# Eleven late stages in one pipeline, and half of a spectrum product on GpSimd

## The chip, the core and the metric

The kernel runs on one core of a Trainium2 chip. The metric is the device time of one execution in microseconds; three runs of the kernel before gave 946.32, 946.88 and 947.59, so the median is 946.88. The core has a matrix engine (TensorE, PE), VectorE (DVE), ScalarE (ACT), GpSimd (POOL) and a queue for transfers (SyncE, SP). Each engine runs its own list of instructions strictly in the order in which it is written. Semaphores carry the dependencies: an instruction that waits holds up everything behind it on its engine.

## The reference

The input is x, 8 samples of 512 positions by 128 channels, float32. Four blocks follow each other, each of the form x = x + layernorm(block(layernorm(x))):

```
# 1: six layers, per layer:
q, k, v = heads(ln(x) @ wq), heads(ln(x) @ wk), heads(ln(x) @ wv)
x = (softmax(q) @ (softmax(k, over positions).T @ v)) @ wo + bo + x
x = leaky_relu(ln(x) @ w1) @ w2 + x
# 2: spiking feed-forward
y = relu(x @ W_fc.T) ** 2 @ W_proj.T
out = (how often a leaky accumulator of y fires in 5 steps) / 5
# 3: a state space convolution
u = (x @ Win.T + bin).T
k = einsum(C * B * dt, exp(-exp(-A_log) * dt * t))     # a kernel of 512 taps per channel
y = irfft(rfft(u, 1024) * rfft(k, 1024))[:512] + u * Dp
out = y.T @ Wout.T + bout
# 4: a gate over a time shift
xr, xk = mu_r * x + (1 - mu_r) * x_prev, mu_k * x + (1 - mu_k) * x_prev
out = sigmoid(xr @ W_r.T) * (relu(xk @ W_k.T) ** 2 @ W_v.T)
```

## The kernel before

A sample is a tile of 128 partitions by 512 (four blocks of 128). Three loops follow each other.

`layers` runs 51 steps. Step n begins item n (48 items: 6 layers by 8 samples), and at the same time carries items n-1, n-2 and n-3 through their later parts, so that the two matrix products with w1 (`h`) and w2 (`y`) of one item lie beside the attention of another.

`pipeline(6, spiking)` runs 14 steps. It holds block 2, and the start of block 3 (u and its eight bands, `butterfly`) for one sample per step. The convolution's own kernel is made here and in the layers: exponents on VectorE (L1144) and ScalarE (L883) in the layers' steps 8 to 24, 64 small products on TensorE (`kernel_slices`) in this loop's first two steps, and its spectrum (`spectrum`) in steps 3 to 10.

`slots` runs 17 steps with up to eight stages in each. It holds the rest of block 3 (`forward`, `inverse`, `out_proj`) and block 4. The transform `forward` takes four samples at a time, so that its products are 512 wide; its four multiplications, its subtraction and its addition per quarter (L1343 to L1349) are all on VectorE.

A normalisation runs over three engines: statistics on VectorE (`stats`), four or two tiny operations on GpSimd with a power among them (`rstd`, L680 to L683, and `mean_rstd`, L688 to L691), and the scaling on ScalarE (`normalise` L856, `scaled` L898). GpSimd adds the result to x (`add_to_x`, L775). Matrix products stand in line 358 and transposes in line 368 of the profile, whatever calls them.

## Time and profile before

| | |
|---|---|
| median of 3 runs | 946.88 us |
| profiled execution: its time, its span | 947.66 us, 945.9 us |
| TensorE busy | 816.8 us (86%) |
| VectorE busy | 703.6 us (74%) |
| ScalarE busy | 598.7 us (63%) |
| GpSimd busy | 424.9 us (45%) |
| granted TensorE clock, mean | 0.927 |

The span is what the trace covers; the time of the execution is 1.8 us more. The page gives busy time per engine for the whole span, and the kernel has parts with different limits, so the windows below part it: layers in their steady state, and all that lies behind them. A row of a timeline gives the start, the time from the first start to the last end of what it merges, and in brackets how long the engine had been idle and what ended that.

### The profile page before, as it was taken

The page shows a single profiled execution, that of the slowest core. Times are in us where ns is not written, and L with a number is a line of the kernel's source. Part 1 is how long each engine was busy: PE and PEld are TensorE (multiplying, and loading weights), DVE is VectorE, ACT ScalarE, POOL GpSimd, SP SyncE. Part 2 cuts the span into 40 slices and gives each one's busy share as a digit, 9 for nine tenths or more (in the row PEclk, how much of TensorE's full clock was granted, in tenths as well). Part 3 has the DMA queues.
Part 4 walks back from the last instruction along what each step waited for, and adds up shares of the span by engine and source line. Part 5 has one row for each costly group of instructions (what it writes and reads, how often), then busy time and mean ns, then how long its engine had stood idle before and what let it go on. Part 6 is the DMA issues. An engine that isn't in the chain of part 4 may idle for free.

```text
span 945.9 us, 15397 instructions
## 1 busy us (share of the span) xinstructions
PE 816.8 (86%) x5085; PEld 689.2 (73%) x5092; DVE 703.6 (74%) x2019; ACT 598.7 (63%) x1275; POOL 424.9 (45%) x706
## 2 busy tenths in 40 slices
PE   2688999999999999999999999989878766888543
PEld 2577878888888888888888888889657643646432
DVE  5788888888888888888888887620456789689843
ACT  3366767777777777777777677531778751236554
...
DMA packets 19726, 13.65 MB, mean 14 GB/s; under 512 B 2488, under 2 KB 18495, under 8 KB 19647
## 3 DMA queue, kind: packets, MB, share of 16 engines
...
## 4 chain that ended last, share of the span: by engine, by line
PE 65%; DVE 13%; ACT 9%; POOL 6%; issue 5%; DMA 0%; POOLq 0%; DVEq 0%; ACTq 0%
PE PS L358 58%; PE PS L368 7%; ACT XR L898 2%; POOL R L683 1%; ACT HL L982 1%; ACT XR L856 1%; ACT EK L856 1%; DVE ST L1098 1%; POOL RSTD L741 1%; DVE STATS L1191 1%; ACT HL L986 1%; DVE XI L1184 1%; POOL QB L757 1%; POOL RSTD L735 1%; POOL X L775 1%
## 5 line engine op out<-in xcount | busy, mean ns | idle before, releaser
L358 PE MATMUL PS<-W,HL 128*128 128x128 f32 x1536 | 201.7, 275 | 0.0
L358 PEld LDWEIGHTS PS<-W,HL 128*128 128x128 f32 x1536 | 193.4, 191 | 8.2
L919 ACT ACTIVATE HL<-PS 128x512 f32<-128x512 f32 x192 | 109.4, 594 | 22.7 <-PE PS L358 18.2
L724 POOL TENSOR_TENSOR JOIN<-STATS 128x8 f32<-128x8 f32 (+1 forms) x50 | 12.9, 257 | 220.5 <-DVE STATS L1191 220.5
L368 PE MATMUL PS<-ID,XR 128*128 128x128 f32 x448 | 73.2, 288 | 33.2 <-ACT XR L856 17.1
L358 PE MATMUL PS<-X2H,W1L 128*128 128x512 f32 x192 | 88.6, 461 | 5.9 <-issue 4.4
L368 PEld LDWEIGHTS PS<-ID,XR 128*128 128x128 f32 x448 | 53.0, 146 | 53.7 <-ACT XR L898 20.1
L939 ACT ACTIVATE EK<-PS,NKM 128x512 f32<-128x512 f32 x48 | 33.1, 689 | 88.1 <-DVE NKM L1261 88.1
L1191 DVE BATCH_NORM_STATS2 STATS<-XI 128x6 f32<-128x128 f32 x384 | 82.5, 278 | 0.3
L763 POOL TENSOR_TENSOR QB<-QB,QRC 128x512 f32<-128x512 f32 x48 | 51.0, 1062 | 69.6 <-DVE QRC L1295 69.6
L898 ACT ACTIVATE XR<-XI,RSTD 128x128 f32<-128x128 f32 x192 | 61.5, 393 | 29.9 <-POOL RSTD L741 29.6
L358 PE MATMUL PS<-X2H,W1H 128*128 128x512 f32 x192 | 75.8, 395 | 0.0
L358 PE MATMUL PS<-X2L,W1H 128*128 128x512 f32 x192 | 75.7, 394 | 0.0
L680 POOL TENSOR_SCALAR VE<-MV 128x4 f32<-128x4 f32 x56 | 13.5, 241 | 124.7 <-DVE MV L1102 68.5
L741 POOL TENSOR_TENSOR RSTD<-JOIN,MHALF 128x4 f32<-128x4 f32 x48 | 64.8, 1349 | 0.1
L358 PE MATMUL PS<-MM,QS 128*128 128x128 f32 x384 | 56.0, 290 | 9.1 <-DVE MM L1242 5.9
L683 POOL TENSOR_TENSOR R<-VE,MHALF 128x4 f32<-128x4 f32 x56 | 58.9, 1053 | 4.7
L358 PEld LDWEIGHTS PS<-MM,QS 128*128 128x128 f32 x384 | 48.1, 197 | 16.8 <-issue 8.5
L1271 DVE STREAM_TRANSPOSE QB<-QF 128x512 f32<-128x512 f32 x48 | 34.1, 711 | 32.9 <-ACT QF L851 32.9
L757 POOL TENSOR_TENSOR QB<-QB,QMX 128x512 f32<-128x512 f32 x48 | 51.1, 1064 | 5.1 <-DVE QMX L1273 5.1
L358 PE MATMUL PS<-EKT,XR 128*128 128x128 f32 x384 | 51.9, 279 | 1.6 <-ACT EKT L851 1.6
L1236 DVE TENSOR_TENSOR XR<-XI,RSTD 128x512 f32<-128x512 f32 x48 | 51.2, 1067 | 0.1
...
## 6 DMA issues: line engine op xcount, KB each, us to landing
...
QKV<-in_qkv SPq DMA_DIRECT2D x6, 192.0 KB, 2.9
...
```

The lines of the kernel that those rows point to most:

```text
L358: return nc.tensor.matmul(o, l, r, start=start, stop=stop, skip_group_check=True)
L368: last = nc.tensor.transpose(o[:, j * P:(j + 1) * P], i[:, j * P:(j + 1) * P], ID[:, :])
L683: return pool.tensor_tensor(r[:, :], ve[:, :], MHALF[:, 0:TILES], ALU.pow)
L741: pool.tensor_tensor(RSTD[:, 0:TILES], JOIN[:, 4, 0:TILES], MHALF[:, 0:TILES], ALU.pow).then_inc(s["ln1_rstd"], 1)
L757: pool.tensor_tensor(heads(QB[:, :]), heads(QB[:, :]), QMX[:, :].unsqueeze(2).broadcast_to([P, 32, DH]), ALU.subtract).then_inc(s["q_sub"], 1)
L763: pool.tensor_tensor(heads(QB[:, :]), heads(QB[:, :]), QRC[:, :].unsqueeze(2).broadcast_to([P, 32, DH]), ALU.mult).then_inc(s["q_nrm"], 1)
L898: last = nc.scalar.activation(o[:, j * P:(j + 1) * P], tile(src, b, j), ACT.Copy, scale=r[:, first + j:first + j + 1])
L919: nc.scalar.activation(HL[f][:, :], pH[f % 2][:, :], ACT.Prelu, alpha=LEAK).then_inc(s["hl"], 1)
L939: nc.scalar.activation(EK[:, :], pK[:, :], ACT.Exp, bias=NKM[:, 0:1], accum_out=KSM[:, 0:1]).then_inc(s["ek"], 1)
L1191: last = nc.vector.bn_stats(STATS[:, first + j, :], tile(XI, b, j))
L1236: tt(tiles(XR2[:, :]), tiles(seq(XI, before(b, 2))), per_tile(RSTD[:, TILES:2 * TILES]), ALU.mult).then_inc(s["xr2"], 1)
L1271: nc.vector.transpose(QB[:, :], QF[:, :]).then_inc(s["q_blk"], 1)
```

## The change

The two loops behind the layers are replaced by one. It has eleven stages, and sample v is in stage k at step 48 + v + k; the first three stages lie in the layers' last three steps, and `late` runs steps 51 to 65. This text calls a step of it t, with t = n - 48, from 0 to 17. The feed-forward of block 2 uses the layers' own `h` and `y` and their normalisation (stages 0 to 3); SPIKE is stage 4, STATE (normalise and transpose for block 3) 5, CONV (u, bands, transform, products) 6, BACK (inverse transform, projection, normalise) 7, SHIFT (normalise and transpose for block 4) 8, GATE 9 and FINISH 10. The constants:

```diff
-CHUNKS = {TABLES + 1 + i: i for i in range(PAIRS // 4)}
-
-SLICES = {0: range(0, 36), 1: range(36, PAIRS)}
-SPECTRUM = {3: (0, 1), 4: (2, 3), 6: (4,), 7: (5,), 8: (6,), 9: (7,), 10: (8,)}
-
-FIRST_SPECTRA = {BATCH + 3: (0, 1), BATCH + 4: (2,), BATCH + 5: (3,)}
-INVERSE, PROJECT, NORM, LN, TURN, MIX, GATE, FINISH = range(8)
-
-STARTS = [0, 1, 2, 3, None, None, 4, 5, 6, 7]
+ADD, PART, TURN, FFN, SPIKE, STATE, CONV, BACK, SHIFT, GATE, FINISH = range(11)
+def sample(n, stage):
+
+    v = n - ITEMS - stage
+    return v if 0 <= v < BATCH else None
+def late(step):
+    for n in range(ITEMS + 3, ITEMS + BATCH + FINISH):
+        step(n)
+CHUNKS = {0: (range(0, 3), range(3, 7)), 1: (range(7, 12), range(12, 16))}
+SLICES = {1: ((0, 8), (8, 14), (14, 20)), 2: ((20, 28), (28, 36), (36, 44)), 3: ((44, 51), (51, 58), (58, 64))}
+CENTRE, CENTRE_IN = ITEMS - 6, ITEMS - 5
+SPECTRUM = {ITEMS - 4: (0, 1, 2, 3), ITEMS - 3: (4, 5, 6, 7), ITEMS - 2: (8,)}
...
```

On TensorE the transform takes one sample, the time shift moves behind the matrices (W times a mix of x and x_prev becomes two products with prepared matrices), and one step is written as follows:

```diff
+def transform(v, n):
+    pe.wait_ge(s["bands"], v + 1)
+    pe.wait_ge(s["kf"], 3)
...
+    for half, bank in enumerate((pK, pW)):
+        for k in range(TILES):
+            for j in range(2):
+                last = mm(bank[:, k * P:(k + 1) * P], FWD[:, j * BINS * P + half * SEQ + k * P:][:, 0:P],
+                          V[:, (2 * k + j) * P:(2 * k + j + 1) * P], j == 0, j == 1)
+        last.then_inc(s["f_ps"], 1)
...
+def key_and_gate(v, n):
...
+    mm(pXT[:, :], WK1[:, :], SH[:, 1:1 + SEQ], True, False)
+    mm(pXT[:, :], WK2[:, :], SH[:, 0:SEQ], False, True).then_inc(s["k2_ps"], 1)
...
+    for j in range(TILES):
+        mm(pQ[:, j * P:(j + 1) * P], SH[:, 1 + j * P:1 + (j + 1) * P], WR1[:, :], True, False)
+        last = mm(pQ[:, j * P:(j + 1) * P], SH[:, j * P:(j + 1) * P], WR2[:, :], False, True)
+    last.then_inc(s["r_ps"], 1)
...
+def late_step(n):
...
+    if conv is not None:
+        project_in(conv, n)
+    if has_m:
+        h(m, 2)
+        y(m, 0)
+    if back is not None:
+        inverse(back)
+    if has_m:
+        y(m, 1)
+        h(m, 3)
+    if gate is not None:
+        key_and_gate(gate, n)
+    if has_m:
+        y(m, 2)
+    if has_x:
+        second_turn(n)
+    if has_m:
+        y(m, 3)
+    if spike is not None:
+        count(spike, n)
+    if conv is not None:
+        transform(conv, n)
+    if gate is not None:
+        value(gate)
+    if back is not None:
+        project_out(back, n)
+    if state is not None:
+        state_turn(state, n)
+    if has_x:
+        h(m + 1, 0)
+    if shift is not None:
+        shift_turn(shift, n)
+    if has_x:
+        h(m + 1, 1)
+late(late_step)
...
```

On GpSimd the convolution kernel's exponents move into the first two steps of the layers, and two of four multiplications of the spectrum come from VectorE, after a copy by ScalarE (`IMAG`):

```diff
+decay()
+exponents(0)
+input_rstd(0)
+exponents(1)
+exponents(2)
+join(0, TILES, 0)
+ln1_power(0)
+input_rstd(1)
+input_rstd(2)
+for p4 in range(3, 7):
+    exponents(p4)
...
+    if n == 0:
+        for p4 in range(7, 9):
+            exponents(p4)
+    if has_n:
+        pool.wait_ge(s["q_rec"], n + 1)
+        pool.tensor_tensor(heads(QB[:, :]), heads(QB[:, :]), QRC[:, :].unsqueeze(2).broadcast_to([P, 32, DH]),
+                           ALU.mult).then_inc(s["q_nrm"], 1)
+    if n == 0:
+        for p4 in range(9, PAIRS // 4):
+            exponents(p4)
+    if n + 3 < BATCH:
+        input_rstd(n + 3)
...
+def late_step(n):
...
+    if shift is not None:
+        pool.wait_ge(s["o_z"], shift + 1)
+        add_to_x(shift, ZOUT[:, :]).then_inc(s["o_x"], 1)
+    if state is not None:
+        pool.wait_ge(s["cnt_z"], state + 1)
+        add_to_x(state, ZCNT[:, :]).then_inc(s["cnt_x"], 1)
+    if shift is not None:
+        pool.wait_ge(s["sh_var"], shift + 1)
...
+        rstd_mean(3, EPS).then_inc(s["sh_nm"], 1)
+    if state is not None:
+        pool.wait_ge(s["st_var"], state + 1)
...
+        rstd(1, EPS).then_inc(s["st_rstd"], 1)
+    join_next(n)
+    if n + 1 < ALL:
+        ln1_power(n + 1)
+    if finish is not None:
+        pool.wait_ge(s["rv_z"], finish + 1)
+        add_to_x(finish, MEM[:, :]).then_inc(s["done"], 1)
+    if spike is not None:
+        pool.wait_ge(s["cnt_var"], spike + 1)
...
+        rstd_mean(0, EPS * STEPS * STEPS).then_inc(s["cnt_nm"], 1)
+    if conv is not None:
+        pool.wait_ge(s["imag"], conv + 1)
...
+        pool.tensor_tensor(PI[:, :], IMAG[:, :], KIM[:, :], ALU.mult).then_inc(s["turned"], 1)
+        pool.tensor_tensor(PR[:, :], IMAG[:, :], KRB[:, :], ALU.mult).then_inc(s["turned"], 1)
+    if gate is not None:
+        pool.wait_ge(s["rv_var"], gate + 1)
...
+        rstd_mean(4, EPS).then_inc(s["rv_nm"], 1)
+    if back is not None:
+        pool.wait_ge(s["o_var"], back + 1)
...
+        rstd_mean(2, EPS).then_inc(s["o_nm"], 1)
+late(late_step)
...
```

On ScalarE the six loads for the convolution kernel are issued first, before any other work, and a late step is written as follows:

```diff
+for t, d in ((ALOG, alog), (DTR, dtr), (IOTA, iota), (BMAT, bmat), (CMAT, cmat), (DP, dp)):
+    act.dma_start(t[:, :], d).then_inc(s["ssm_in"], 16)
+act.wait_ge(s["ssm_in"], SSM_LOADS)
+nc.scalar.activation(LA[:, :], ALOG[:, :], ACT.Exp, scale=-1.0).then_inc(s["la_exp"], 1)
+keys_high(0)
...
+def late_step(n):
...
+    if has_m:
+        hl(m, 0)
+        hl(m, 1)
+        hl(m, 2)
+    if finish is not None:
+        act.wait_ge(s["rv_nm"], finish + 1)
...
+        normalise(MEM[:, :], ACC[:, :], RS[4], NMS[4]).then_inc(s["rv_z"], 1)
+    if back is not None:
+        act.wait_ge(s["inv_ps"], back + 1)
...
+        copy(YR[:, :], pW[:, 2 * P:4 * P])
+        copy(YS[:, :], pK[:, 2 * P:4 * P]).then_inc(s["second"], 1)
+    if has_m:
+        hl(m, 3)
+    if state is not None:
+        act.wait_ge(s["st_rstd"], state + 1)
...
+        scaled(XS, state, 0, X, RS[1]).then_inc(s["st_x"], 1)
+    if gate is not None:
+        act.wait_ge(s["k2_ps"], gate + 1)
+        nc.scalar.activation(RK[:, :], pXT[:, :], ACT.Relu).then_inc(s["r_relu"], 1)
+        act.wait_ge(s["r_relu"], gate + 1)
...
+        nc.scalar.activation(SQ[:, :], RK[:, :], ACT.Square).then_inc(s["r_sq"], 1)
+        act.wait_ge(s["r_ps"], gate + 1)
...
+        nc.scalar.activation(SIG[:, :], pQ[:, :], ACT.Sigmoid).then_inc(s["r_sig"], 1)
+    if has_x:
+        second_copy(n)
+    if shift is not None:
+        act.wait_ge(s["sh_nm"], shift + 1)
...
+        normalise(ZN[:, :], lambda j: tile(X, shift, j), RS[3], NMS[3]).then_inc(s["sh_z"], 1)
+    if has_m:
+        act.wait_ge(s["y_ps"], (m + 1) * FB)
...
+        copy(YM[:, :], pY[:, :]).then_inc(s["ym"], 1)
+    if spike is not None:
+        act.wait_ge(s["cnt_nm"], spike + 1)
...
+        normalise(ZCNT[:, :], pQ[:, :], RS[0], NMS[0]).then_inc(s["cnt_z"], 1)
+    if state is not None:
+        act.wait_ge(s["st_T_ps"], state + 1)
...
+        copy(XTS[:, :], pX2[:, :]).then_inc(s["st_T"], 1)
+    if shift is not None:
+        act.wait_ge(s["sh_T_ps"], shift + 1)
+        act.wait_ge(s["sh0"], 1)
...
+        copy(SH[:, 1:1 + SEQ], pX2[:, :]).then_inc(s["sh_T"], 1)
+    if conv is not None:
+        act.wait_ge(s["f_ps"], 2 * conv + 2)
...
+        copy(IMAG[:, :], pW[:, :]).then_inc(s["imag"], 1)
+    if back is not None:
+        act.wait_ge(s["o_nm"], back + 1)
...
+        normalise(ZOUT[:, :], YO[:, :], RS[2], NMS[2]).then_inc(s["o_z"], 1)
+    if n + 1 < ALL:
+        next_input(n)
+late(late_step)
...
```

On VectorE:

```diff
+def products(v):
+    yr, yi = YF[:, 0:SEQ], YF[:, SEQ:2 * SEQ]
+    dve.wait_ge(s["f_ps"], 2 * v + 1)
...
+    tt(yr, pK[:, :], KRE[:, :], ALU.mult).then_inc(s["f_part"], 1)
+    tt(yi, pK[:, :], KIM[:, :], ALU.mult).then_inc(s["f_part"], 1)
+    dve.wait_ge(s["f_part"], 2 * v + 2)
+    dve.wait_ge(s["turned"], 2 * v + 2)
+    tt(yr, yr, PI[:, :], ALU.subtract)
+    tt(yi, yi, PR[:, :], ALU.add).then_inc(s["spectra"], 1)
...
+def late_step(n):
...
+    if has_x:
+        second_scale(n)
+    if n < ALL:
+        add_norm(n)
+    if shift is not None:
...
+        stats(lambda j: tile(X, shift, j), 3).then_inc(s["sh_var"], 1)
+    if state is not None:
...
+        stats(lambda j: tile(X, state, j), 1).then_inc(s["st_var"], 1)
+    if n <= ALL:
+        part_stats(n)
+    if conv is not None:
+        bands(conv)
+    if spike is not None:
+        spikes(spike)
+    if back is not None:
+        back_bands(back)
+    if has_x:
+        second_low(n)
+    if spike is not None:
...
+        stats(lambda j: pQ[:, j * P:(j + 1) * P], 0).then_inc(s["cnt_var"], 1)
+    if n + 2 < ALL:
+        first_stats(n)
+    if gate is not None:
...
+        tt(ACC[:, :], pXT[:, :], SIG[:, :], ALU.mult).then_inc(s["rv"], 1)
...
+        stats(lambda j: ACC[:, j * P:(j + 1) * P], 4).then_inc(s["rv_var"], 1)
+    if back is not None:
...
+        tt(tiles(YO[:, :]), tiles(pXT[:, :]), BOUT[:, :].unsqueeze(1).broadcast_to([P, TILES, P]),
+           ALU.add).then_inc(s["o_sum"], 1)
...
+        stats(lambda j: YO[:, j * P:(j + 1) * P], 2).then_inc(s["o_var"], 1)
+    if conv is not None:
+        products(conv)
+late(late_step)
```

`hl` of a late item is now a Relu and a Square. `next_input` scales XR for the coming step. The 64 small products of the convolution kernel lie in the layers' steps 1 to 3, its spectrum in steps 44 to 46, the centring of two matrices in 42 and 43. The names of the order below: BIG holds V, YF, ZCNT, ZOUT, ZN, XS, XTS, YT, YO, RK, SQ, SIG, PI and PR in the kernel after, QF holds YM, QS holds IMAG and EK holds MEM.

ScalarE, the end of a spiking step before (it ends with the normalisation of the spike count, EK):

```order
L898 ACTIVATE QS<-X,R 128x128 x4
L982 ACTIVATE HL<-PS 128x512
L986 ACTIVATE HL<-HL 128x512
L898 ACTIVATE XR<-X,R 128x128 x4
L982 ACTIVATE HL<-PS 128x512
L986 ACTIVATE HL<-HL 128x512
L851 ACTIVATE X2H<-PS 128x512
L851 ACTIVATE XTF<-PS 128x512
L856 ACTIVATE XR<-XI,NM,R 128x128 x4
L851 ACTIVATE YM<-PS 128x512
L856 ACTIVATE EK<-PS,NM,R 128x128 x4
```

ScalarE, the end of step t = 9 after: the spike count's normalisation, the transposed state (BIG<-PS), SH, IMAG (QS<-PS), the normalisation of block 3's output (BIG<-BIG), and then the next step's first Relu and Square:

```order
L828 ACTIVATE BIG<-PS,NM,R 128x128 x4
L823 ACTIVATE BIG<-PS 128x512
L823 ACTIVATE SH<-PS 128x512
L823 ACTIVATE QS<-PS 128x512
L828 ACTIVATE BIG<-BIG,NM,R 128x128 x4
L883 ACTIVATE HA<-PS 128x512
L886 ACTIVATE HL<-HA 128x512
L883 ACTIVATE HA<-PS 128x512
L886 ACTIVATE HL<-HA 128x512
```

What moved: between two feed-forward pairs now stand the end of five samples' stages, and the last of them waits for GpSimd.

GpSimd, the layers' step 0 into step 1, before (QB is the softmax of q, JOIN the statistics of the next step):

```order
L763 TENSOR_TENSOR QB<-QB,QRC 128x512
L711 TENSOR_SCALAR VEX<-MVX 128x4
L714 TENSOR_TENSOR RX<-VEX,MHALF 128x4
L705 TENSOR_TENSOR W1L<-W,W1H 128x512
L724 TENSOR_TENSOR JOIN<-STATS 128x8
L725 TENSOR_TENSOR JOIN<-STATS 128x8
L727 TENSOR_TENSOR JOIN<-JOIN 128x8
L728 TENSOR_SCALAR JOIN<-JOIN 128x8
```

GpSimd, the same place after:

```order
L754 TENSOR_TENSOR QB<-QB,QRC 128x512
L664 TENSOR_TENSOR BIG<-LA,IOTA 128x512 x7
L685 TENSOR_SCALAR VEX<-MVX 128x4
L688 TENSOR_TENSOR RX<-VEX,MHALF 128x4
L679 TENSOR_TENSOR W1L<-W,W1H 128x512
L698 TENSOR_TENSOR JOIN<-STATS 128x8
```

What moved: seven exponents, each 128 by 512 (BIG<-LA,IOTA), stand between the end of step 0 and the statistics of step 1.

## Rows read from the trace of the kernel before

**Rows 1.** Windows: stretch, its us, busy us (x instructions) of each engine, clock, DMA share, GB/s.
```profile
19.85:62.90 43.05, 30.19 (x139) 23.88 (x138) 34.36 (x104) 20.17 (x44) 20.71 (x33) 0.72 0.19 61
...
112.00:590.00 478.00, 472.21 (x3269) 414.24 (x3268) 396.66 (x949) 360.31 (x747) 233.19 (x374) 1.00 0.03 8
...
627.00:946.00 319.00, 229.79 (x1116) 176.77 (x1121) 202.20 (x774) 158.67 (x368) 131.31 (x224) 0.82 0.03 7
```

**Rows 2.** Waits of 673 to 946 us: waiter, released by: us in all, times, longest.
```profile
PE PS L358 <- ACT EK L856: 18.5, 7, 4.4
```

**Rows 3.** Timeline, ScalarE, 715 to 738 us: start, us, instruction, idle before.
```profile
720.84 1.50 ACT L856 ACTIVATE EK<-PS,NM,R 128x128 f32<-128x128 f32 x4
...
725.30 0.60 ACT L982 ACTIVATE HL<-PS 128x512 f32<-128x512 f32 x1 [2.96 <-PE PS L358]
...
725.93 0.63 ACT L986 ACTIVATE HL<-HL 128x512 f32<-128x512 f32 x1
...
735.34 1.50 ACT L856 ACTIVATE EK<-PS,NM,R 128x128 f32<-128x128 f32 x4
```

**Rows 4.** Timeline, TensorE, 728 to 731 us.
```profile
728.30 1.05 PE L358 MATMUL PS<-PROJ,HL 128*128 128x128 f32 x8
...
729.11 0.48 PE L358 MATMUL PS<-X2H,FCL 128*128 128x512 f32 x1
...
729.89 0.60 PE L368 MATMUL PS<-ID,QS 128*128 128x128 f32 x4
...
730.32 0.94 PE L358 MATMUL PS<-PROJ,HL 128*128 128x128 f32 x7
```

**Rows 5.** Timeline, GpSimd and VectorE, 720 to 724 us.
```profile
720.54 1.27 POOL L775 TENSOR_TENSOR X<-X,XR 128x512 f32<-128x512 f32 x1 [3.51 <-ACT XR L856]
...
720.91 1.18 DVE L1209 TENSOR_TENSOR FLY<-U 128x256 f32<-128x256 f32 x1
...
722.01 0.41 DVE L1210 TENSOR_TENSOR FLY<-U 128x256 f32<-128x256 f32 x1
```

**Rows 6.** Timeline, GpSimd, the first 36 us.
```profile
5.18 0.19 POOL L711 TENSOR_SCALAR VEX<-MVX 128x4 f32<-128x4 f32 x1 [3.90 <-DVE MVX L1178]
...
28.86 1.06 POOL L763 TENSOR_TENSOR QB<-QB,QRC 128x512 f32<-128x512 f32 x1 [5.38 <-DVE QRC L1295]
...
35.62 0.21 POOL L724 TENSOR_TENSOR JOIN<-STATS 128x8 f32<-128x8 f32 x1 [2.71 <-DVE STATS L1191]
```

**Rows 7.** The page, part 6: one DMA issue, KB, us to landing.
```profile
QKV<-in_qkv SPq DMA_DIRECT2D x6, 192.0 KB, 2.9
```

**Rows 8.** Groups of instructions: line, form, count, busy us, mean ns, idle before.
```profile
L358 PE MATMUL PS<-CE,BIG 128*128 128x8 f32 x128 | 27.0, 357 | 0.4 <-ACT WINC L851 0.4
```

**Rows 9.** Timeline, VectorE line 1299 (second residual), single instructions.
```profile
119.33 0.63 DVE L1299 TENSOR_TENSOR XI<-PS,XI 128x512 f32<-128x512 f32 x1
...
170.69 0.63 DVE L1299 TENSOR_TENSOR XI<-PS,XI 128x512 f32<-128x512 f32 x1
...
218.16 0.63 DVE L1299 TENSOR_TENSOR XI<-PS,XI 128x512 f32<-128x512 f32 x1
...
267.19 0.63 DVE L1299 TENSOR_TENSOR XI<-PS,XI 128x512 f32<-128x512 f32 x1
...
627.26 0.69 DVE L1299 TENSOR_TENSOR XI<-PS,XI 128x512 f32<-128x512 f32 x1 [6.46 <-PE PS L358]
```

**Rows 10.** Timeline, TensorE, VectorE and GpSimd, 924 to 940 us.
```profile
924.47 1.92 PE L358 MATMUL PS<-QS,WKT 128*128 128x512 f32 x2
...
936.16 0.69 DVE L1481 TENSOR_TENSOR ACC<-PS,QB 128x512 f32<-128x512 f32 x1 [3.75 <-ACT MEM L856]
...
936.88 0.87 DVE L1098 BATCH_NORM_STATS2 ST<-ACC 128x6 f32<-128x128 f32 x4
...
938.25 0.19 POOL L680 TENSOR_SCALAR VE<-MV 128x4 f32<-128x4 f32 x1 [0.88 <-DVE MV L1102]
...
939.92 0.19 POOL L691 TENSOR_SCALAR NM<-NM 128x4 f32<-128x4 f32 x1
```

More of the change, by code:

```diff
@@ L1 @@
+import itertools
 import numpy as np
@@ L29 @@
 ITEMS = LAYERS * BATCH
+ALL = ITEMS + BATCH
 def spike_levels():
@@ new lines, in second_turn, with kernel_slices @@
+            def second_turn(n):
+                pe.wait_ge(s["xr2"], n - 1)
+                if passed(n - 1, SHIFT):
+                    pe.wait_ge(s["sh_T"], passed(n - 1, SHIFT))
+                transposes(pX2, XR2).then_inc(s["x2T_ps"], 1)
+            def kernel_slices(first, end):
+                pe.wait_ge(s["bm_out"], 1)
+                pe.wait_ge(s["ce1"], 1)
+                pe.wait_ge(s["e2"], -(-end // 4))
+                for i in range(first, end):
+                    last = mm(pW[:, i * 8:i * 8 + 8], E2[:, i * P:(i + 1) * P], CE1[:, i * 8:i * 8 + 8])
+                if end == PAIRS:
+                    last.then_inc(s["k_ps"], 1)
```

1142 lines of the change are left out of this document (441 added, 701 removed).

## The prediction

> **What bounds the kernel now.** I read windows first, then waits, then timelines. The layers' steady state is bound by TensorE: in 112 to 590 us it is busy 472 of 478 us at full clock [rows 1]. So there work taken from VectorE or ScalarE gives nothing, and work added to TensorE costs its full length. The last residual of the layers is added at 627.3 us [rows 9], which leaves 318.6 us of the span of 945.9. There no engine is full: TensorE 230 of 319 us at a clock of 0.82, VectorE 202, ScalarE 159, GpSimd 131 [rows 1]. That part is bound by chains through four engines in fixed order. The plainest one: in the spiking steps TensorE waits 18.5 us in seven steps for ScalarE's normalisation of the count [rows 2]; one such normalisation starts at 720.84 and the next at 735.34, so a step is 14.5 us, although no engine has 14.5 us of work in it [rows 3]. By hand that chain is: normalisation 1.5, two products with FCH until the first Relu can start 0.8, four pairs of Relu and Square at 1.26, two scalings of about 1.3, two copies and YM at 0.6, a normalisation of 1.6: 13.3 us. The trace has 14.5, 9% more, from hand-overs and from TensorE at its lower level of 1.2 GHz after an idle stretch (ScalarE waits 2.96 us for the first h there). I keep this 9% as the surcharge on every chain below.
>
> **What the change does, by part.** I split it into the front (to the last residual) and the late part.
>
> Front, first normalisation. GpSimd starts it at 5.18 us [rows 6]. Now `decay` and one exponent come first. They wait for six loads from ScalarE's queue; a load lands some 2.9 us after its issue [rows 7], and with six issues in a row that is an estimated 6.2 us. Then an Exp, seven small GpSimd operations (0.2 to 0.3 each, 1.9) and an exponent of 1.06, the time of a 128x512 operation with a broadcast operand on GpSimd (QB in [rows 6]): 9.5 us. Nothing covers it, since everything waits for the first sample: +4.3.
>
> Front, step 1. The softmax product ends at 29.9 and the statistics are joined at 35.6 [rows 6]. Seven exponents (7.4) then stand in between, with the input's power (1.2) and W1L (1.6): 29.9 + 10.2 = 40.1 against 35.6, less what small slack VectorE has (0.5): +4.0. Behind this GpSimd work wait q_sub, the power for XR, and through them TensorE's next transposes.
>
> Front, the 64 small products. They take 27.0 us at the low clock (0.42 each) [rows 8], and about half of that at the high one. They move into steps 1 to 3, where TensorE is busy 30.2 of 43.1 us [rows 1]: 13 idle us, but in short waits on the path. Bounds: 0 if all fits, 14 if none. I take +5, and nothing back for a warmer clock. In step 6 the butterfly of the taps comes onto a VectorE that has little slack there: +1.5.
>
> Front, steps 42 to 46. 18 products of 128x128 for the spectrum (0.20 each, from four in 0.81 [rows 4]), one 512 wide (0.85) and one small, on a full TensorE: 4.7, and 0.6 for three copies ahead of GT on ScalarE: +5.3.
>
> Front, what goes. The steps that held the decay took 51.4 us for four steps (119.33 to 170.69), the same four of the next layer 49.0 [rows 9]: -2.3. The other exponents lay in steps bound by TensorE: 0. Sum of the front: 4.3 + 4.0 + 5 + 1.5 + 5.3 - 2.3 = +17.8; bounds +8 and +27.
>
> Late part. It replaces 31 steps by 18, of which 3 lie beside the layers' end. Loads of the fullest step, t = 9: VectorE about 22 us, TensorE about 22, ScalarE 19, GpSimd 19. But the order closes one cycle through all of it. From the end of a first Square (H): h and y 1.6; `inverse`, eight products of twice the width, 3.2; y, h 1.6; `key_and_gate` 2 x 0.85 + 8 x 0.20 = 3.3; y, transposes, y 2.05; count 1.2; `transform` 16 x 0.20 = 3.2; `value` 0.8; ACC on VectorE 0.7 (`project_out` writes the bank that ACC reads); `project_out` 0.8; state transposes, h, shift transposes 0.43 + 0.78 + 0.43 (TensorE in [rows 4], ACC in [rows 10]). That is 20.1. Then ScalarE: SH 0.6 and IMAG 0.6, for IMAG stands behind SH and so behind the shift transposes, though `transform` ended 5 us earlier. GpSimd: two products of 1.27 [rows 5], then, in its order, the gate's `rstd_mean` and the output's, 1.85 each (938.25 to 940.1) [rows 10]. ScalarE: ZOUT 1.6, and only then the next step's Relu and Square 1.26 [rows 3], for which TensorE's h waits. Sum 31.5 with hand-overs of 1 us: 9 us over the load of any engine.
>
> The other steps by the same walk: t = 3 only h, y and X2: 8.7. t = 4, 5, 6: the count's statistics (1.25), `rstd_mean`, ZCNT and XR stand between y and the next Relu: 14, 14.5, 15. t = 7 and 8: `back_bands` (four of 0.41, six of half that: 2.8) stands on VectorE behind `bands` (3.2 by the same rows, [rows 5]) and the five thresholds (1.8), and `transform` waits for it: 26, 25.5. t = 9: 31.5. t = 10: 29. From t = 11 there is no feed-forward, and the cycle goes on from ZOUT through `add_to_x` and the statistics to `bands`: 27, 25.5, 23.5. t = 14: 12.5. Tail of the last sample: add and statistics 2.5, `rstd_mean` 1.85, normalise, transpose, SH 2.7, `key_and_gate` at 1.2 GHz (WKT once takes 1.7 there [rows 10], so 3.4 + 3.4), `value` 1.1, and ACC to the end of the span 945.9 - 936.16 = 9.7 [rows 10]: 25. Head, from 627.3 to the first Square: 2. Sum 280; with 9%: 305 in place of 318.6, a gain of 13.5. Bounds: 280 with no surcharge; 330 with 18%, if TensorE falls to 1.2 GHz in each long gap of t = 4 to 6 and 11 to 13.
>
> The two spectrum products on GpSimd. VectorE's product takes 0.7 and its multiplications at this place are no bottleneck; GpSimd's 2.5 for both stand on the cycle, in steps t = 7 to 13. VectorE would do both in 1.2 without waiting for IMAG: 1.9 us less in each of seven steps.
>
> The Trainium skill ("GPSIMD Engine Reference", section Engine selection) says that elementwise two-input work belongs on VectorE, being about twice as slow on GpSimd. The trace agrees (1.27 against 0.7). By that rule, with the products left on VectorE, the sum would be some 13 us lower.
>
> A GpSimd operation also slows VectorE operations with two operands in SBUF: FLY takes 1.18 us beside `add_to_x` and its twin just after it 0.41 [rows 5]. There is more large GpSimd work now, some of it beside `bands`: 0 to 0.8 us a step, in the surcharge.
>
> **Sum.** 627.3 + 17.8 + 305 = 950.1 of span, and 1.8 around it: 951.9, against 947.66 of the same profiled execution. The median of the runs is 0.8 lower, so about 951. No difference is within 0.2%, 945.0 to 948.8, which is about what a measurement can tell.
>
> **Rivals.** (a) Not slower: TensorE stays warm. Its work is denser, 22 of 31 us in the full steps, and if the clock is 2.4 GHz nearly throughout, the surcharge falls to 3% (288) and the small products fill idle time in steps 1 to 3 (front +10): 627.3 + 10 + 288 + 1 = 926. Against it: 72% was busy in the late part before as well, and the clock was 0.82 [rows 1]. (b) The cycle isn't closed as I read it, because waits that I take for true are met early; then steps go by load (20, 20.5, 22, 22, 20, 17, 15 for t = 7 to 13, in place of 188): 51 us less, 900. Against it: ScalarE's list is a fixed order and ZOUT really stands ahead of the first Relu. (c) Worse: low clock in all gaps and GpSimd beside VectorE: late part 325, front +22: 975. For it: three of the steps leave TensorE idle for some 8 us each. It decides where the late part exceeds the old 318.6. (d) That the products don't move off VectorE's load or the stages don't overlap at all is excluded by the order of the instructions.
>
> **Chances.** Forecast (943 to 966) 0.53, (a) 0.24, (b) 0.06, (c) 0.17. Faster: (a), (b) and 0.03 of the forecast, 0.33. Same: 0.09 of the forecast and no other. Slower: the other 0.41 and (c), 0.58. The range 929 to 972 leaves out (b), the lower third of (a) and a third of (c).
>
> **What will show it.** The first XR on ScalarE near 15.5 us in place of 11.3; the last residual of the layers (L1299 before) near 645. In step t = 9 IMAG starts after SH; TensorE waits some 7 us or more before the h that follows the first Square, released by ScalarE; the distance between two ZOUT is 27 to 34 us there; VectorE is idle for 5 us or more ahead of the shift statistics, released by GpSimd's add. GpSimd shows 16 products of 1.27. If instead ScalarE never waits for NM in front of ZOUT for more than 1 us, or the layers end before 635, the prediction is wrong.

## The result, and the profile after

The changed kernel takes 969.88 us (median of four runs, 968.31 to 971.57), the one before 946.6 beside it: ratio 1.0241, 95% interval 1.0228 to 1.0255. It is 23 us slower; I had forecast 951, 4 us slower. The time lies inside the range of 929 to 972, at its upper end; the direction was right and the size was not. The profiled execution has a span of 967.7 us. One execution of the run taps_later below took 1389.09 us at a mean granted clock of 0.56; it is slow by itself and left out of its figures.

Where the layers end is read from the second residual on VectorE (L1294 here, L1299 before, [rows 9]):

```profile
659.36 0.69 DVE L1294 TENSOR_TENSOR XI<-PS,XI 128x512 f32<-128x512 f32 x1 [0.41 <-PE PS L312]
```

659.36 against 627.26: the front is 32.1 us longer, where I had 17.8. The rest of the span is 308.3 us, where I had 305, against 318.6 before. So the late part came out as worked out, and the error lies in the front. The windows say the same (the columns are those of [rows 1]; the changed kernel first, then the first 110 us of the kernel before):

```profile
0.00:110.00 110.00, 77.92 (x437) 70.71 (x438) 71.19 (x218) 50.40 (x107) 59.33 (x98) 0.81 0.23 68
112.00:590.00 478.00, 468.43 (x3234) 411.95 (x3233) 388.24 (x935) 349.72 (x727) 228.37 (x366) 1.00 0.03 8
...
659.00:967.00 308.00, 213.79 (x1223) 176.01 (x1222) 166.62 (x632) 143.41 (x322) 133.78 (x228) 0.86 0.03 8
```
```profile
0.00:110.00 110.00, 77.69 (x453) 65.96 (x453) 85.61 (x260) 58.97 (x123) 51.98 (x93) 0.89 0.24 68
```

The middle is TensorE's as before; in the first 110 us its clock is 0.81, before it was 0.89. In the last 308 us TensorE is busy 214, and no other engine more than 167: chains, not load.

**The cycle of step t = 9.** ScalarE, GpSimd, TensorE and VectorE, from their timelines:

```profile
792.40 1.50 ACT L828 ACTIVATE BIG<-PS,NM,R 128x128 f32<-128x128 f32 x4 [2.15 <-POOL NM L648]
...
797.51 0.60 ACT L823 ACTIVATE SH<-PS 128x512 f32<-128x512 f32 x1 [0.81 <-PE PS L322]
798.01 0.59 ACT L823 ACTIVATE QS<-PS 128x512 f32<-128x512 f32 x1
805.36 1.65 ACT L828 ACTIVATE BIG<-BIG,NM,R 128x128 f32<-128x128 f32 x4 [6.76 <-POOL NM L648]
806.91 0.57 ACT L883 ACTIVATE HA<-PS 128x512 f32<-128x512 f32 x1
```
```profile
798.68 1.26 POOL L804 TENSOR_TENSOR BIG<-QS,KIM 128x512 f32<-128x512 f32 x1 [6.32 <-ACT QS L823]
799.90 1.26 POOL L805 TENSOR_TENSOR BIG<-QS,KRB 128x512 f32<-128x512 f32 x1
801.25 0.19 POOL L641 TENSOR_SCALAR VE<-MV 128x4 f32<-128x4 f32 x1
...
803.48 0.19 POOL L641 TENSOR_SCALAR VE<-MV 128x4 f32<-128x4 f32 x1
```
```profile
808.20 0.79 PE L312 MATMUL PS<-X2H,FCL 128*128 128x512 f32 x1 [9.13 <-ACT HL L886]
```
```profile
801.90 0.68 DVE L1338 TENSOR_TENSOR BIG<-BIG 128x512 f32<-128x512 f32 x1
808.38 0.87 DVE L1074 BATCH_NORM_STATS2 ST<-X 128x6 f32<-128x128 f32 x4 [5.81 <-POOL X L769]
```

Read them in order: IMAG (its buffer is QS) starts at 798.01, straight behind SH; the two products follow; then the gate's powers (801.25) and the output's (803.48); ZOUT at 805.36, after 6.76 us of waiting; the Relu at 806.91; TensorE's h at 808.20, after 9.13 us. The spectra are complete at 802.6, and VectorE then waits 5.81 us for the addition to x. The signs that I had named for this step are there, with 35.0 us from the ZOUT before (it starts at 770.36) to this one and 34.1 to the next, where I had 27 to 34. The two signs of the front are not: the first XR starts at 17.53 us and not near 15.5, and the last residual lies at 659 and not near 645.

The length of a late step is the distance between two starts of ScalarE's copy YR, from t to t + 1. The experiments' steps stand below it, in us; the late part runs from the last residual of the layers to the end of the span:

| from t = | 7 | 8 | 9 | 10 | 11 | 12 | 13 | sum | late part |
|---|---|---|---|---|---|---|---|---|---|
| forecast with 9% | 28.3 | 27.8 | 34.3 | 31.6 | 29.4 | 27.8 | 25.6 | 205 | 305 |
| changed kernel | 29.4 | 27.9 | 34.6 | 28.1 | 30.8 | 28.4 | 28.1 | 207 | 308.3 |
| pool_order | 28.2 | 26.8 | 28.7 | 31.1 | 28.0 | 24.7 | 26.0 | 193 | 295.4 |
| imag_first | 28.5 | 25.0 | 30.6 | 24.5 | 27.2 | 24.4 | 24.3 | 184 | 287.3 |
| vector_products | 23.9 | 23.5 | 30.0 | 25.7 | 25.2 | 23.6 | 23.2 | 175 | 278.1 |
| relu_first | 21.3 | 29.0 | 32.8 | 30.2 | 30.8 | 29.0 | 26.5 | 200 | 298.1 |
| vp_relu | 21.7 | 26.0 | 24.8 | 27.4 | 23.6 | 26.9 | 23.3 | 174 | 269.7 |

**The front.** One row of each step is enough, the transpose of q on VectorE (step 0, 1, 4, 5 and 6; before in the first fence, after in the second):

```profile
19.85 0.71 DVE L1271 STREAM_TRANSPOSE QB<-QF 128x512 f32<-128x512 f32 x1 [1.33 <-ACT QF L851]
36.10 0.71 DVE L1271 STREAM_TRANSPOSE QB<-QF 128x512 f32<-128x512 f32 x1 [0.56 <-ACT QF L851]
...
76.36 0.71 DVE L1271 STREAM_TRANSPOSE QB<-QF 128x512 f32<-128x512 f32 x1 [0.75 <-ACT QF L851]
89.69 0.71 DVE L1271 STREAM_TRANSPOSE QB<-QF 128x512 f32<-128x512 f32 x1 [0.75 <-ACT QF L851]
102.41 0.71 DVE L1271 STREAM_TRANSPOSE QB<-QF 128x512 f32<-128x512 f32 x1 [0.75 <-ACT QF L851]
```
```profile
26.61 0.71 DVE L1266 STREAM_TRANSPOSE QB<-QF 128x512 f32<-128x512 f32 x1 [1.33 <-ACT QF L823]
46.84 0.71 DVE L1266 STREAM_TRANSPOSE QB<-QF 128x512 f32<-128x512 f32 x1 [0.55 <-ACT QF L823]
...
98.17 0.71 DVE L1266 STREAM_TRANSPOSE QB<-QF 128x512 f32<-128x512 f32 x1 [0.74 <-ACT QF L823]
111.47 0.71 DVE L1266 STREAM_TRANSPOSE QB<-QF 128x512 f32<-128x512 f32 x1 [0.74 <-ACT QF L823]
128.36 0.71 DVE L1266 STREAM_TRANSPOSE QB<-QF 128x512 f32<-128x512 f32 x1 [0.74 <-ACT QF L823]
```

| term | forecast | measured |
|---|---|---|
| first normalisation | +4.3 | +6.8 |
| step 0 to 1 | +4.0 | +4.0 |
| steps 1 to 4 (small products) | +5 | +11.1 |
| butterfly, step 5 to 6 | +1.5 | +4.2 |
| what goes (steps 6 to 42) | -2.3 | -1.3 |
| steps 42 to 46 | +5.3 | +5.6 |
| last three steps, to the last residual | 0 | +1.8 |

A single trace doesn't fix these figures to the last microsecond. Five of the runs below (pool_order, vector_products, imag_first, relu_first, vp_relu) have the changed kernel's front unchanged. In their traces step 0 to 1 is 20.2 us each time, but steps 1 to 4 are 7.9 to 10.1 us longer than before and not 11.1, step 5 to 6 takes 17.0 to 18.4 us, and the last residual lies between 656.1 and 659.5. The clock is part of it. Six of the small products of step 1, in the changed kernel (first, granted clock 0.50 there) and in vector_products (clock 1.00):

```profile
45.86 2.56 PE L312 MATMUL PS<-CE,BIG 128*128 128x8 f32 x12
```
```profile
45.84 1.40 PE L312 MATMUL PS<-CE,BIG 128*128 128x8 f32 x12
```

So a difference of less than 3.4 us between two last residuals is assigned to an edit only where the step that it touches shows it.

### The profile page after: what moved, and what is told of

It reads as the page before. It is cut to its first block, busy times and chain, and to the rows that moved or that the text cites. A ratio compares the mean times of both kernels' runs of the same rounds, so it can differ in the third digit from the quotient of the medians.

```text
span 967.7 us, 15901 instructions
## 1 busy us (share of the span) xinstructions
PE 826.9 (85%) x5364; PEld 718.4 (74%) x5364; DVE 674.1 (70%) x1903; ACT 590.1 (61%) x1252; POOL 452.0 (47%) x753
## 4 chain that ended last, share of the span: by engine, by line
PE 67%; POOL 11%; issue 10%; DVE 8%; ACT 4%; DMA 0%; ACTq 0%; POOLq 0%; DVEq 0%
PE PS L312 59%; PE PS L322 7%; POOL R L642 3%; ACT XR L867 1%; POOL RSTD L715 1%; DVE ST L1074 1%; POOL BIG L804 1%; POOL BIG L805 1%; DVE STATS L1149 1%; ACT BIG L828 1%; POOL RSTD L709 1%; POOL X L769 1%; POOL QB L746 1%; DVE XI L1142 1%; DVE XI L1256 1%
## 5 line engine op out<-in xcount | busy, mean ns | idle before, releaser
L698 POOL TENSOR_TENSOR JOIN<-STATS 128x8 f32<-128x8 f32 (+1 forms) x58 | 15.4, 266 | 237.2 <-DVE STATS L1149 237.2
L867 ACT ACTIVATE XR<-XI,RSTD 128x128 f32<-128x128 f32 x224 | 71.7, 396 | 32.9 <-POOL RSTD L715 29.7
L1149 DVE BATCH_NORM_STATS2 STATS<-XI 128x6 f32<-128x128 f32 x416 | 89.4, 278 | 1.9 <-POOL JOIN L699 1.5
L322 PE MATMUL PS<-ID,XR 128*128 128x128 f32 x416 | 65.5, 281 | 20.5 <-ACT XR L867 20.3
L322 PEld LDWEIGHTS PS<-ID,XR 128*128 128x128 f32 x416 | 48.8, 143 | 36.3 <-issue 18.9
L715 POOL TENSOR_TENSOR RSTD<-JOIN,MHALF 128x4 f32<-128x4 f32 x56 | 71.7, 1280 | 0.1
L312 PEld LDWEIGHTS PS<-MM,QS 128*128 128x128 f32 x384 | 49.0, 200 | 15.5 <-issue 9.0
L709 POOL TENSOR_TENSOR RSTD<-JOIN,MHALF 128x4 f32<-128x4 f32 x56 | 56.5, 1010 | 4.5 <-POOL JOIN L704 0.2
L1256 DVE TENSOR_TENSOR XI<-PS,XI 128x512 f32<-128x512 f32 x48 | 33.2, 692 | 34.0 <-PE PS L312 34.0
L312 PE MATMUL PS<-INV,BIG 128*128 128x256 f32 x128 | 40.5, 486 | 18.7 <-DVE BIG L1338 18.7
L872 ACT ACTIVATE XTH<-PS,LNC,SC 128x512 fp32r<-128x512 f32 x48 | 37.3, 778 | 24.2 <-PE PS L322 24.2
```

Source lines behind the costliest of these rows:

```text
L312: return nc.tensor.matmul(o, l, r, start=start, stop=stop, skip_group_check=True)
L322: last = nc.tensor.transpose(o[:, j * P:(j + 1) * P], i[:, j * P:(j + 1) * P], ID[:, :])
L709: pool.tensor_tensor(RSTD[:, TILES:end], JOIN[:, 4, TILES:end], MHALF[:, TILES:end], ALU.pow).then_inc(s["ln2_rstd"], 1)
L715: power = pool.tensor_tensor(RSTD[:, 0:TILES], JOIN[:, 4, 0:TILES], MHALF[:, 0:TILES], ALU.pow)
L867: last = nc.scalar.activation(o[:, j * P:(j + 1) * P], tile(src, b, j), ACT.Copy, scale=r[:, first + j:first + j + 1])
L872: return nc.scalar.activation(o[:, :], i[:, :], ACT.Identity, scale=SC[slot][:, which:which + 1], bias=LNC[slot][:, 2 * which + 1:2 * whic ...
```

## The experiments

A ratio is against the kernel before, from runs on the same chip, with its 95% interval; "less" is against the changed kernel's 969.88. The diffs are shortened: a call of several lines stands in one, and the "..." are mine.

**pool_order, vector_products, imag_first: the late cycle.**

```diff
 # pool_order: the two products (turned) behind the powers
+rstd_mean(4, EPS) ... rstd_mean(2, EPS)
 pool.tensor_tensor(PI, IMAG, KIM); pool.tensor_tensor(PR, IMAG, KRB)
-rstd_mean(4, EPS) ... rstd_mean(2, EPS)
 # vector_products: no IMAG, no turned; in products(v)
+tt(PI[:, :], pW[:, :], KIM[:, :], ALU.mult)
+tt(PR[:, :], pW[:, :], KRB[:, :], ALU.mult)
 # imag_first, on ScalarE
 normalise(ZCNT, ...)
+copy(IMAG[:, :], pW[:, :])
 copy(XTS, ...); copy(SH, ...)
-copy(IMAG[:, :], pW[:, :])
```

> The changed kernel, with one edit: on GpSimd the two spectrum products of a late step stand behind the gate's and the output's rstd_mean instead of in front of them. Theory 1 (a cycle through GpSimd's fixed order): in the changed kernel ZOUT of step t = 9 waits 6.8 us for NM, and the output's statistics were there at 797.7, its powers only at 803.5; without the products in front, ZOUT starts about 5.5 us earlier in each of t = 9 to 13 and 3 us in t = 7 and 8: 33 us less, some 937 us (927 to 948). Theory 2 (the late steps are limited by the clock and by the engines' work, GpSimd's order hides behind it): 965 to 970. Nothing changes ahead of the last residual of the layers (659 us).

954.34 us (ratio 1.0077, 1.0052 to 1.0103): 15.5 less, half of what I expected. The order moved one wait into another. In its own t = 9:

```profile
798.10 1.26 POOL L814 TENSOR_TENSOR BIG<-QS,KIM 128x512 f32<-128x512 f32 x1
799.32 1.26 POOL L815 TENSOR_TENSOR BIG<-QS,KRB 128x512 f32<-128x512 f32 x1
800.54 2.95 POOL L769 TENSOR_TENSOR X<-X,BIG 128x512 f32<-128x512 f32 x2
```

The additions to x now follow the products without a gap, and VectorE's last two spectrum operations run beside them at more than twice their length:

```profile
800.68 1.68 DVE L1337 TENSOR_TENSOR BIG<-BIG 128x512 f32<-128x512 f32 x1 [3.30 <-POOL BIG L815]
802.28 1.76 DVE L1338 TENSOR_TENSOR BIG<-BIG 128x512 f32<-128x512 f32 x1
```

From the start of IMAG to the end of the spectra it is 7.5 us (796.53 to 804.04), in the changed kernel 4.6. TensorE's waits from 720 to 930 us, the changed kernel first:

```profile
PE PS L312 <- ACT HL L886: 23.1, 3, 9.1
PE PS L312 <- DVE BIG L1338: 18.7, 5, 5.2
```
```profile
PE PS L312 <- DVE BIG L1338: 29.7, 5, 8.4
PE PS L312 <- ACT HL L886: 11.0, 3, 4.2
```

> The changed kernel, with one edit: VectorE makes all four spectrum products from PSUM, GpSimd none, and ScalarE's copy of the imaginary half is gone. Theory 1 (what costs is that GpSimd's powers stand behind a wait for ScalarE's copy and two products): as with the order alone, 33 us less, within 4 us of it, since VectorE's 1.3 us more per step take the place of the wait for GpSimd. Theory 2 (the products' own 1.27 us against 0.68 is what costs, as my prediction priced it: 1.9 us in seven steps): 13 us less, 957. Theory 3 (VectorE is full, so the move pays): slower than the changed kernel, 975.

939.46 us (ratio 0.9921, 0.9894 to 0.9949): 30.4 less, so this one version is already 0.8% faster than the kernel before. The first theory has the size (33 us) and not the reason: it asked for as much from the order alone, which gave 15.5. The second theory, my own price of 13 us, is less than half of it.

> The changed kernel, with one edit: ScalarE's copy of the imaginary half (IMAG) stands behind ZCNT and in front of XTS and SH, instead of behind SH. In t = 9 transform ends at 792.7, the copy runs at 798.0. Theory 1 (two cycles: GpSimd's powers behind its products hold ZOUT, and the products hold the spectra that the next inverse transform waits for; the order on GpSimd alone gave 15.5 us because it shortened the first and lengthened the second): the copy 4 us earlier shortens both, so 3.5 us less in each of t = 7 to 13, 20 to 25 us less: 947 (944 to 951), more than the GpSimd order gave. Theory 2 (what ends last is VectorE's list or TensorE's clock): under 10 us less, over 960.

947.21 us (ratio 1.0006, 0.9986 to 1.0027): 22.7 less, as the first theory said (20 to 25), and no difference from the kernel before. One copy, moved two places up a list, is worth as much as the whole change cost:

```profile
788.82 1.50 ACT L828 ACTIVATE BIG<-PS,NM,R 128x128 f32<-128x128 f32 x4 [2.15 <-POOL NM L648]
790.20 0.61 ACT L823 ACTIVATE QS<-PS 128x512 f32<-128x512 f32 x1
...
798.07 1.65 ACT L828 ACTIVATE BIG<-BIG,NM,R 128x128 f32<-128x128 f32 x4 [3.53 <-POOL NM L648]
```

From ZCNT to ZOUT it is 9.25 us here, 12.96 in the changed kernel. TensorE's two waits are both shorter, 16.4 us for HL (23.1) and 10.1 for L1338 (18.7). The three runs together: GpSimd's products sit on two cycles at once, in front of the powers (ZOUT) and in front of the spectra (inverse); an edit must shorten both.

**relu_first, vp_relu: ScalarE's order at the step's border.** The first two pairs of Relu and Square of the next step go ahead of ZOUT (ahead of ZCNT for t = 3 to 5).

```diff
+if has_x: hl(m + 1, 0); hl(m + 1, 1)
 normalise(ZOUT, ...)      # end of step n
-hl(m, 0); hl(m, 1)        # start of step n + 1
 hl(m, 2)
```

> The changed kernel, with one edit on ScalarE: the first two pairs of Relu and Square of the next step stand in front of ZOUT (from t = 6) or of ZCNT (t = 3 to 5) instead of behind them. GpSimd's order stays. Theory 1 (my prediction's cycle: ZOUT stands ahead of the first Relu, and TensorE's h waits 9.1 us for it in t = 9): h starts 5 to 6 us earlier and the inverse transform then waits for the spectra of 802.6, so 2.5 to 4 us less in each of t = 7 to 10, and 2 us in each of t = 4 and 5: 14 us less, 956 (951 to 961). Theory 2 (the spectra, and behind them GpSimd's products, close another cycle that is as long): under 4 us less, 966 to 970. From t = 11 nothing changes by either, there is no feed-forward.

957.29 us (ratio 1.0116, 1.0087 to 1.0145): 12.6 less, near the first theory's 14. But in the traces only 10.2 of it lie in the late part (308.3 to 298.1); the other 3.2 lie in the front, which the edit doesn't touch (step 1 to 2 17.15 us in place of 18.57, step 2 to 3 15.58 in place of 17.37). And it came less evenly than expected: step 7 gave 8 us, step 8 lost 1, the way to t = 7 gave 3.

> The changed kernel with all four products on VectorE and the first Relu pairs ahead of ZCNT and ZOUT, the front untouched. It separates the late part of the best version from its front. Theory 1 (the late gains add: 30.4 and 12.6): 927. Theory 2 (with the products on VectorE the spectra are ready early and the Relu pairs give more than alone): 922. Theory 3 (they overlap): 934. The best version's late part took 915.8 - 647.0 = 268.8 us against 278.1 with the products alone, so I expect 659.4 + 268.8 + 1.8 = 930.

929.56 us (ratio 0.9794, 0.9764 to 0.9825): 9.9 less than vector_products, 8.4 by the late parts (278.1 to 269.7). The gains add, nearly.

**coeff, no_slices, start, no_taps_work: what the taps cost in the front.**

```diff
 # coeff
-if n == 0: coefficients()
 value_mask(layer)
+if n == 0: coefficients()
 # no_slices
-for i in range(first, end): last = mm(pW[:, i*8:i*8+8], E2[...], CE1[...])
+if end == PAIRS: last = mm(pW[:, :], E2[:, 0:P], E2[:, 0:SEQ])
 # start
-decay(); exponents(0); input_rstd(0); ...
+input_rstd(0); decay(); join(0, TILES, 0); ...
+EXPONENTS = {0: range(1, 5), 1: range(5, 9), 2: range(9, 12), 3: range(12, 15), 4: range(15, 16)}
```

> The changed kernel, with one edit: VectorE's two operations for the small products' coefficients (CE, 2.0 us) stand behind the value mask of step 0 instead of in front of the centring of wo. My prediction didn't count them. Theory 1 (they are on the path in step 0, since TensorE waits 5.1 us for MBV in place of 3.1): the first step takes 18.0 to 18.3 us in place of 20.2, the last residual comes near 656.5, the time 967.5. Theory 2 (only the exponents on GpSimd make step 0 long, as I predicted): no change within 1 us, since QRC's product on GpSimd and the joining of statistics are what the next step waits for.

970.77 us (ratio 1.0249, 1.0217 to 1.0281): nothing in the time, and the last residual is at 659.65. But where the edit acts it gives 1.3 us: step 0 to 1 took 18.95 us in place of 20.2. GpSimd's softmax product waits for VectorE's QRC, which stands behind the coefficients, and the seven exponents stand behind that product; it starts 1.25 us earlier (changed kernel first):

```profile
37.67 1.06 POOL L754 TENSOR_TENSOR QB<-QB,QRC 128x512 f32<-128x512 f32 x1 [5.25 <-DVE QRC L1290]
```
```profile
36.42 1.06 POOL L754 TENSOR_TENSOR QB<-QB,QRC 128x512 f32<-128x512 f32 x1 [4.15 <-DVE QRC L1290]
```

The next four steps are as in the changed kernel to 0.1 us. What takes the gain away is step 5 to 6, 18.45 us at a clock of 0.82 in place of 16.89 at 0.90; vector_products, with the coefficients where they were, has 18.42 at 0.81 there. So neither theory holds as it stands: the first asked for 2 us, the second for none, and the coefficients are on the path for 1.3.

> The changed kernel without the 64 small products of the convolution kernel: one product of 128x512 stands in their place, so its taps are not the reference's. This measures the term that I put at 5 us and that shows as 11.1 us in steps 2 to 4. Theory 1 (TensorE is full there and every small product costs its length): 11 us less in steps 2 to 4, and 2 to 4 of step 1, last residual near 646, time 956 to 959. Theory 2 (the steps are long because TensorE has fallen to 1.2 GHz after the long wait for the first sample, and the products fill idle time): 3 to 6 us less, 965.

964.76 us (ratio 1.0189, 1.0156 to 1.0223). The last residual is at 651.97, 7.4 us earlier, between the two theories: 1.6 of it in step 0 to 1, 1.1 in step 1 to 2, 3.2 in step 2 to 3 and 2.0 in step 3 to 4, less 0.3 in step 5 to 6. Against the five traces with the same front it is 4.1 to 7.6 us. TensorE is busy for 21.2 us with the small products in the changed kernel, so about a third of their length is exposed. The time, 5.1 less, is the second theory's only because the same late part took 313.3 us.

> The changed kernel, with the convolution kernel's exponents spread out: the first normalisation goes first on GpSimd, the 16 exponents come one after it and then up to four in each of the layers' steps 0 to 4 in front of the softmax product, ScalarE's powers up to a step later, and the 64 small products in steps 2 to 6 (they were in steps 1 to 3), the copy and butterfly of the taps in step 7. Theory 1: first softmax transpose on VectorE at 20.3 (26.6 in the changed kernel, 19.9 before), step 1 takes 16.5 us (20.2), and the small products cost 6 to 8 us in place of 11, since TensorE is at 2.4 GHz for more of them: last residual of the layers near 645 in place of 659, the time 956 (951 to 961). Theory 2 (TensorE's clock stays low because of the products, wherever they stand): the first 10 us are gained and 5 of them lost again, 965.

961.05 us (ratio 1.0156, 1.0128 to 1.0184): 8.8 less. The first transpose came at 20.18 as expected, but step 0 to 1 still took 19.4 us. Steps 1 to 6, with the small products and the rest of the exponents in them, are 9.0 us longer than before; in the changed kernel steps 1 to 4 are 11.1 longer, 7.9 to 10.1 in the five traces with its front. Spread over five steps the work is hardly hidden better than in three.

> The changed kernel without the making of the convolution kernel's taps: no exponents, no powers, no coefficients, one 128x512 product in place of 64 small ones (the taps are not the reference's); the butterfly and the spectrum stay. This closes the sum of the front: 32.1 us more than before. Theory 1 (the whole loss of the front is work of the taps in steps 0 to 7, plus butterfly 4.2, spectrum 5.6, conversion of full size 1.8, less 2): last residual near 627.3 + 9.6 = 637, the late part unchanged at 308 to 310, the time 947. Theory 2 (the three loads first on ScalarE's queue, or the order of the other work, cost a part of it): above 641.

953.65 us (ratio 1.0062, 1.0046 to 1.0078). Last residual at 640.08: making the taps costs 19.3 us of the front (16.0 to 19.4 by the five traces with the same front), where my terms (4.3, 4.0, 5) gave 13.3. The other 12.8 us are butterfly, spectrum, the last steps and 1.6 in step 2 to 3. These 1.6 aren't the one product that stands in for the 64, which runs at 65.97, behind that step. They come with the clock, 0.88 there and 0.98 before: products of 512 columns take 0.63 us and before 0.39. I had expected 947: 3 us of the rest are the front's, 3 the late part's, 312.7 us.

The two runs together show the backlog of GpSimd. In step 1 to 2 ScalarE waits for GpSimd's part of the softmax where the exponents are made (no_slices, first), and hardly where they aren't (no_taps_work); that step takes 17.5 us in the one and 14.2 in the other, 14.1 before:

```profile
52.37 0.63 ACT L971 ACTIVATE QB<-QB 128x512 f32<-128x512 f32 x1 [3.82 <-POOL QB L746]
```
```profile
39.70 0.63 ACT L950 ACTIVATE QB<-QB 128x512 f32<-128x512 f32 x1 [0.47 <-POOL QB L738]
```

The same late code takes 308 to 313 us in six traces. Between the changed kernel and no_taps_work 4.3 us differ: 2.0 up to t = 7, 1.8 in the step from t = 7, 0.5 behind t = 14. That step in the changed kernel (first) and in no_taps_work:

```profile
723.50:752.80 29.30, 20.54 (x123) 17.83 (x122) 21.39 (x83) 11.70 (x26) 16.14 (x30) 0.83 0.00 1
```
```profile
706.20:737.30 31.10, 22.26 (x122) 19.60 (x123) 21.58 (x84) 11.74 (x26) 16.11 (x30) 0.78 0.00 1
```

Work and order are equal; the granted clock is 0.78 in place of 0.83, and TensorE's busy time 1.7 us longer. So with an edit of the front the late part can differ by up to 5 us without being touched, and the front by up to 3.4 with an edit of the late part; medians alone would book that on the edit. Whether the edit brings it about or chance does, no run separates.

**taps_later: the butterfly.** It is cut in five pieces, one each in steps 9 to 13 in front of the wait for the context product.

```diff
-if n == BATCH - 2: butterfly(KTM, KV)          # ahead of second_scale
+if 0 <= n - BATCH - 1 < 5: taps(n - BATCH - 1)  # ahead of the wait for c_ps
```

> The changed kernel, with the butterfly of the taps (4.2 us on VectorE at the start of step 6) cut in five pieces of 0.6 to 0.8 us, one each in steps 9 to 13 in front of the wait for the context product. Theory 1 (VectorE's list is in order and XR2 and MM stand behind it, so all of it is on the path in step 6, and TensorE, idle for it, falls to 1.2 GHz once): step 6 takes 12.8 us in place of 16.9, steps 9 to 13 are 11.9 to 14.2 as before: 4.0 us less, 965.9. Theory 2 (my prediction: only 1.5 of it is exposed): 1.5 us less, 968.4.

965.09 us (median of three, ratio 1.0202, 1.0168 to 1.0236): 4.8 less. Step 5 to 6 took 13.02 us in place of 16.89, and steps 9 to 13 are within 0.1 us of what they were: 3.9 us of the 4.2. In it are both the wait and the clock, which is 0.90 in that step in the changed kernel and 1.00 here. In the changed kernel TensorE waits 2.7 us there for MM, which stands behind the butterfly:

```profile
PE PS L312 <- DVE MM L1244: 2.7, 1, 2.7
```

The last residual moved by 6.5, since step 1 to 2 took 17.2 in place of 18.6 and step 2 to 3 15.8 in place of 17.4 as well, which the edit doesn't touch.

**best1, best2: faster versions.** Both hold vector_products and relu_first; they differ in where the taps are made.

```diff
 # best1: start, coeff and taps_later, with
+EXPONENTS = {0: range(1, 4), 1: range(4, 6), 2: range(6, 9), 3: range(9, 12), 4: range(12, 15), 5: range(15, 16)}
+SLICES = {3: ((0, 6), (6, 11), (11, 16)), ..., 6: ((48, 54), (54, 59), (59, 64))}
 # best2: one exponent and one power a step in steps 10 to 26, loads on SP's queue, and
+LATE_SLICES = {51: ((0, 8), (8, 16), (16, 24), (24, 40)), 52: ((40, 52), (52, 64))}
+if n == 53: spectrum(0) ... spectrum(7)
+if n == 54: spectrum(8)
```

> A version meant to beat both kernels: the changed kernel with all four products on VectorE, the first Relu pairs ahead of ZCNT and ZOUT, the first normalisation first on GpSimd, exponents two or three a step in steps 0 to 5, small products in steps 3 to 6, coefficients behind the value mask, butterfly in five pieces in steps 9 to 13. Theory 1 (the parts add up): front as long as before but for spectrum and the full-size conversion, last residual near 638 (21 us less than 659); products 30 us less, Relu 8 us less: 911 (903 to 920). Theory 2 (they overlap, since each removes a wait of the same step): 925.

918.11 us (ratio 0.9706, 0.9677 to 0.9736). It does all of the work, and is 28 us under the kernel before and 52 under the change. Its late part takes 268.8 us, its last residual is at 647.0 and not at 638: the making of the taps in steps 2 to 7 (most of the exponents, the small products, the copy) costs 11 us there: those steps take 75.1 in place of 64.1.

> A second version meant to beat both: the late part as in the best one so far, but the making of the taps goes back into steps bound by TensorE (one GpSimd exponent a step in steps 10 to 25, one ScalarE power a step behind it), the 64 small products into steps t = 3 and 4, where TensorE is idle 14 of 64 us until t = 6, the butterfly behind the count's statistics of t = 4, the spectrum into t = 5 and 6. Theory 1 (work is free where its engine waits): last residual at 629 to 631 in place of 647, and 6 to 10 us more in t = 3 to 6: 909 (904 to 914). Theory 2 (the small products stand in front of the feed-forward's y in those steps and lengthen the chain by their full 14 us, and the butterfly and spectrum by 5): 920.

926.6 us (ratio 0.9782, 0.9752 to 0.9812). The last residual is at 632.26, 14.8 us earlier than in best1, nearly as expected; but the way from there to t = 7 takes 82.7 us, in vp_relu 58.2. TensorE's idle time in t = 3 to 6 is idle time in a chain, and what is put in it lengthens the chain: the second theory, and more than it.

## Why the prediction was right and wrong

**The late part was right in its steps, and its mechanism in one of two cycles.** 305 worked out, 308.3 measured; the seven full steps 205 and 207. Walking through the fixed order of four engines, with measured durations, gave the cycle to within 2% in sum and 4 us in a single step (t = 10: 31.6 and 28.1). The 9% for hand-overs and clock held in the sum (10% measured); single steps lay from 3% under the walk to 20% over it, and some luck is in how these cancel. The cycle through the powers, ZOUT and the first Relu is there (9.13 us of waiting, 10.2 us from relu_first). What the walk lacked is the second cycle, from IMAG through GpSimd's products to the spectra that the next inverse transform waits for (18.7 us from 720 to 930 us); it is why pool_order gave half of what I expected from it.

**The front failed: +17.8 forecast, +32.1 measured. Of the 14.3 us missing, 8.8 lie in the two terms that were sized by idle time.** (1) "The 64 small products, +5": steps 1 to 4 took 11.1 more (7.9 to 10.1 in the five traces with the same front). Without the small products 6.2 of it go. 3.2 more go without the rest of the taps' making: that is GpSimd's backlog of exponents, which I had counted for one step only. 1.6 stay, with the lower clock in step 2 to 3. (2) "Butterfly +1.5, on a VectorE that has little slack": all of it was exposed, since XR2 and MM stand behind it; taps_later shows 3.9 of the 4.2. (3) "First normalisation +4.3": 6.8. I had the wait (VectorE's normalisation started 4.8 us later) and not the 2.0 us that two VectorE operations there gained in length (1.45 in the normalisation, shown below, and 0.54 in XTL). (4) The last steps, which carry the first stages of the new pipeline, I had at 0, and they cost 1.8; no run takes that apart. (5) "What goes, -2.3" gave 1.3. The term of step 1 was right in size (4.0) by luck: I had put all of it to GpSimd's exponents, but 1.3 us of it go with the coefficients moved (coeff) and 1.6 without the small products (no_slices); without the taps' making 0.3 is left.

**The price of the products was wrong, and it changed no sum.** I said that VectorE would save 1.9 us in each of seven steps, 13 in all. It saves 30: not only the 2.5 us of the products but also the wait for IMAG, the powers queued behind it and the spectra. The row for that was in the forecast's own cycle (IMAG behind SH, 5 us late), and I didn't carry it into this term. The Trainium skill ("GPSIMD Engine Reference", section Engine selection) pointed the right way; its factor of two accounts for 1.2 us a step (1.27 against 0.68 us for each of two products), and what waits for them for the rest.

**The rivals.** (a) asked for a warm TensorE and a late part of 288: the clock there was 0.86 and the part 308. (b) asked for steps by load: refuted by the row at 805.36. (c) came nearest in time (975), and by the wrong part: its late part of 325 did not come, and its front of +22 was too short by 10. Of the two things that it named, GpSimd beside VectorE is in the front, where VectorE lost 2.0 us in the first normalisation. The lower clock isn't shown: the first 110 us have 0.81 in the changed kernel's trace and 0.84 to 0.92 in the five with the same front, 0.89 before.
